# The last cross-attention on explicit keys and values with tiled matmuls, and keys laid out by place modulo 16

## The reference

```
q = xn @ Wq;  k, v = split(ctx @ Wkv)            # 128 -> 1024 = 16 heads x 64
k = concat([nk, k]);  v = concat([nv, v])        # the null key and value
q = l2norm(q) * q_scale;  k = l2norm(k) * k_scale
sim = einsum('bhid,bhjd->bhij', q, k) * 8
out = einsum('bhij,bhjd->bhid', softmax(sim), v)
return layer_norm(out @ Wout, g_out)
```

## Time and profile before

| | |
|---|---|
| median of 3 executions | 1432.56 us (1431.87 to 1434.22) |
| the profiled execution, first to last instruction (span) | 1431.2 us |
| what lies around the span, against the median | 1.4 us |
| PE busy | 1246.7 us, 87% |
| DVE, ACT, POOL busy | 643.0, 439.2, 314.3 us |

### The profile page before, as it was taken

How to read it: one execution, slowest core, us unless ns; L and a number is a source line. 1 busy time by engine, 2 the same in 40 slices (tenths; PEclk the granted TensorE clock), 3 DMA queues, 4 the chain that set the end, 5 groups by cost and what they waited for, 6 DMA issues and landing times.

```text
span 1431.2 us, 12934 instructions
## 1 busy us (share of the span) xinstructions
PE 1246.7 (87%) x4726; PEld 723.7 (51%) x4726; DVE 643.0 (45%) x1098; ACT 439.2 (31%) x550; POOL 314.3 (22%) x94
## 2 busy tenths in 40 slices
PE   7999768896969998777598699999999999999558
PEld 5766423462656664345278444445445444543534
DVE  2167666214447885522342334344444343443334
ACT  2255340431326554033210432222232222223011
POOL 0000000000000000000000046664664566466000
PEclk8799869996689999689689799999999999999569
DMA  8000000002000002001400000000000000000100
GB/s 350 33 1 0 1 0 0 0 1 118 0 1 1 1 1 89 0 0 37 184 1 1 0 8 22 18 15 16 19 20 14 17 21 15 15 19 7 59 7 7
DMA packets 21365, 40.02 MB, mean 28 GB/s; under 512 B 2496, under 2 KB 18880, under 8 KB 19648
## 3 DMA queue, kind: packets, MB, share of 16 engines
q1 hardware_dynamic: 21312, 39.30, 7.4%
HBM read 39.03 MB, written 0.26 MB: 27 GB/s over the span
## 4 chain that ended last, share of the span: by engine, by line
PE 80%; DVE 11%; ACT 5%; issue 2%; POOL 1%; DMA 0%; POOLq 0%; DVEq 0%; ACTq 0%
PE PSUM L1814 15%; PE PSUM L1818 15%; PE PSUM L1389 8%; PE PSUM L1460 4%; PE PSUM L1398 3%; PE PSUM L1421 3%; PE PSUM L1451 2%; PE PSUM L1549 2%; PE PSUM L1560 2%; PE PSUM L1474 2%; PE PSUM L1415 2%; PE PSUM L1849 1%; PE PSUM L1924 1%; DVE ARENA L867 1%; PE PSUM L1843 1%
## 5 line engine op out<-in xcount | busy, mean ns | idle before, releaser
L420 POOL TENSOR_TENSOR ARENA<-ARENA 128x2048 f32<-128x2048 f32 x64 | 288.7, 4510 | 196.5 <-ACT ARENA L654 196.5
L1230 DVE TENSOR_TENSOR ARENA<-PSUM,RK 128x512 f32<-128x512 f32 x256 | 175.5, 690 | 272.5 <-PE PSUM L1814 270.1
L1814 PE MATMUL PSUM<-ARENA,CK 128*128 128x512 f32 x512 | 258.5, 608 | 5.2 <-DVE ARENA L1230 4.2
L1818 PE MATMUL PSUM<-ARENA,CK 128*128 128x512 f32 x512 | 253.8, 598 | 5.8 <-ACT ARENA L676 3.7
L654 ACT ACTIVATE ARENA<-ARENA,CK 128x2048 f32<-128x2048 f32 x64 | 128.1, 2002 | 349.8 <-DVE ARENA L1230 349.8
L1818 PEld LDWEIGHTS PSUM<-ARENA,CK 128*128 128x128 f32 x512 | 97.5, 191 | 131.9 <-issue 113.4
L1814 PEld LDWEIGHTS PSUM<-ARENA,CK 128*128 128x128 f32 x512 | 98.1, 195 | 127.9 <-issue 97.7
L363 POOL TENSOR_TENSOR RSTD<-VE,MHALF 128x4 f32<-128x4 f32 x17 | 17.1, 1009 | 612.3 <-DVE VE L721 612.3
L1389 PE MATMUL PSUM<-WK,CT 128*128 128x512 f32 x256 | 122.4, 600 | 0.0
L450 ACT ACTIVATE SQ<-PSUM 128x512 f32<-128x512 f32 x128 | 76.3, 597 | 83.5 <-PE PSUM L1389 75.7
L743 DVE TENSOR_REDUCE RK<-SQ 128x8 f32<-128x512 f32 x128 | 84.0, 681 | 14.2 <-ACT SQ L450 12.2
(11 more groups left out here) (362 smaller groups left out, 1576.3 us busy)
## 6 DMA issues: line engine op xcount, KB each, us to landing
CT<-in_ctxT SPq DMA_DIRECT2D x4, 1024.0 KB, 10.2
CK<-in_l0f_experts SPq DMA_DIRECT2D x1, 4096.0 KB, 22.8
CK<-in_ctxk SPq DMA_DIRECT2D x1, 4096.0 KB, 12.2
ARENA<-in_l2f_experts SPq DMA_DIRECT2D x2, 2048.0 KB, 8.1
CK<-in_ctxT SPq DMA_DIRECT2D x64, 64.0 KB, 1.7
CK<-in_ctxr SPq DMA_DIRECT2D x64, 64.0 KB, 1.8
ARENA<-in_l2f_experts SPq DMA_DIRECT2D x1, 3072.0 KB, 14.1
WB<-in_wb SPq DMA_DIRECT2D x1, 2738.5 KB, 11.2
```

Source lines behind the costliest of these rows:

```text
L420: nc.gpsimd.tensor_tensor(LS[b % 2], LS[b % 2], PR[:, k % 2, :], ALU.add)\
L1230: ve.tensor_tensor(PR[:, k % 2, c * 512:(c + 1) * 512].rearrange("p (j n) -> p j n", j=4), PSUM[:, c % 2, :].rearrange("p (j n) -> p j n", ...
L1814: mm(bank(c % 2), CTT[:, k, :], qpb[:, b, c * 512:(c + 1) * 512], start=True, stop=True)\
L1818: return mm(bank(4 + c), CKT[:, k, :], PR[:, k % 2, c * 512:(c + 1) * 512], start=first, stop=final, skip_group_check=True)
```

## The change

It does seven things.

1. **Order of the context rows.** Within a batch, row 16m + s now stands at place 128s + m. `CTB` and `KSB` become contiguous: a head's 128 rows are neighbours. The mask is laid out likewise.
2. **No key-norm passes** in the two cores: L1389, L450, L743 go, and the square root and reciprocal of RK with them.
3. **No folded queries** (L1802, L650) and no loads of context tiles in the last block; it reads CT, which no other block overwrites now.
4. **Explicit keys.** For each group of four tiles (512 rows) 8 matmuls of 512 columns (`key_rows`), each copied by ACT into KG and squared by ACT into KSQ. Then 8 matmuls with 32 output rows each (`add_squares`, one per 128 inner features, placed in four column strips of PE) sum the squares, DVE copies them (`key_norms`), four transposes turn them (`turn_norms`), DVE copies 128x64 into RK, and POOL raises 128x64 to -0.5 (`key_scales`).
5. **Explicit values.** Two matmuls of 512 columns for each tile (`value_rows`), copied by DVE.
6. **Tiled matmuls.** Scores of a tile are 16 matmuls of 64 rows, 128 columns, heads 2c and 2c+1 in the upper and the lower 64 rows of PE, into different banks; values are 16 matmuls of 64 output rows, alternately in the two column halves of PE, accumulated in banks 6 and 7, already turned, so `finish_values` and `finish_turn` go. The null key and value are matmuls as well.
7. **The loop** of 64 tiles is written out. Banks 2 to 5 hold scores, 6 and 7 values; all else takes banks 0 and 1 in turn.

The core of the diff:

```diff
+        CTB = CT[:, :].rearrange("p (b s m) -> p b s m", b=B, s=H)
+        KSB = KS.rearrange("p (b s m) -> p b s m", b=B, s=H)
...
+            def key_scales(g):
+                nc.gpsimd.wait_ge(sem("l3x_squares_turned"), PO.due("l3x_squares_turned"))
+                nc.gpsimd.tensor_tensor(RK[:, g % 2, :], RK[:, g % 2, :], MHALF[:, :], ALU.pow)\
+                    .then_inc(sem("l3x_key_scales"), PO.sends("l3x_key_scales"))
+            key_scales(0)
+            for t in range(TILES):
+                b = t // KEY_TILES
+                if t % KEY_TILES == 0:
+                    nc.gpsimd.wait_ge(sem("l3x_l_begun"), PO.due("l3x_l_begun"))
+                nc.gpsimd.wait_ge(sem("l3x_probs"), PO.due("l3x_probs", n=2))
+                nc.gpsimd.tensor_tensor(LS[b % 2], LS[b % 2], PR[:, t % 2, :], ALU.add)\
+                    .then_inc(sem("l3x_summed"), PO.sends("l3x_summed"))
+                nc.gpsimd.wait_ge(sem("l3x_summed"), PO.sent("l3x_summed"))
+                if norm_work(t):
+                    key_scales(t // 4 + 1)
...
+            def probs(t, half):
+                nc.scalar.wait_ge(sem("l3x_scores_taken"), AC.due("l3x_scores_taken", n=2))
+                p = PR[:, t % 2, half * 1024:(half + 1) * 1024]
+                act(p, p, ACT.Exp, bias=SHIFT).then_inc(sem("l3x_probs"), AC.sends("l3x_probs"))
+            probs(0, 0)
+            probs(0, 1)
+            for t in range(TILES):
+                keys = key_work(t)
+                if t and t % KEY_TILES == 0:
+                    nc.scalar.wait_ge(sem("l3x_values"), t)
+                    nc.scalar.wait_ge(sem("l3x_out_kept"), t // KEY_TILES - 1)
+                    act(OT8, PSUM[:, 6:8, :].rearrange("p c n -> p (c n)"), ACT.Copy).then_inc(sem("l3x_o_kept"), AC.sends("l3x_o_kept"))
+                if keys:
+                    key_rows(*keys[0])
+                if t + 1 < TILES:
+                    probs(t + 1, 0)
+                for k in keys[1:]:
+                    key_rows(*k)
+                if keys:
+                    key_squares(*keys[0])
+                if t + 1 < TILES:
+                    probs(t + 1, 1)
+                for k in keys[1:]:
+                    key_squares(*k)
...
+            def key_norms(g):
+                nc.vector.wait_ge(sem("l3x_squares_added"), DV.due("l3x_squares_added"))
+                ve.tensor_scalar(NRM[:, :], bank(work_n[g]), 1e-24, None, ALU.max).then_inc(sem("l3x_squares_kept"), DV.sends("l3x_squares_kept"))
+            def key_norms_turned(g):
+                nc.vector.wait_ge(sem("l3x_norms_turned"), DV.due("l3x_norms_turned"))
+                if g >= 2:
+                    nc.vector.wait_ge(sem("l3x_scores_taken"), 16 * (g - 1))
+                src = PSUM[:, work_t[g], :].rearrange("p (t j r) -> p (t j) r", t=4, j=4)[:, :, 0:4]
+                ve.tensor_copy(RK[:, g % 2, :].rearrange("p (a r) -> p a r", r=4), src)\
+                    .then_inc(sem("l3x_squares_turned"), DV.sends("l3x_squares_turned"))
+            def scale(t, q):
+                k = t % 2
+                if q % 2 == 0:
+                    nc.vector.wait_ge(sem("l3x_scores"), 2 * t + q // 2 + 1)
+                if q == 0:
+                    if t >= 2:
+                        nc.vector.wait_ge(sem("l3x_values"), t - 1)
+                        nc.vector.wait_ge(sem("l3x_summed"), t - 1)
+                    if t % 4 == 0:
+                        nc.vector.wait_ge(sem("l3x_key_scales"), t // 4 + 1)
+                r, i = q // 2, q % 2
+                rk = RK[:, (t // 4) % 2, :].rearrange("p (t j x) -> p t j x", t=4, j=4)[:, t % 4, :, 2 * r + i]
+                ve.tensor_tensor(PR[:, k, q * 512:(q + 1) * 512].rearrange("p (j n) -> p j n", j=4),
+                                 PSUM[:, 2 + q, :].rearrange("p (j n) -> p j n", j=4), each(rk, P), ALU.mult)\
+                    .then_inc(sem("l3x_scores_taken"), DV.sends("l3x_scores_taken"))
+            def value_rows(t, half):
+                nc.vector.wait_ge(sem("l3x_value_rows"), DV.due("l3x_value_rows"))
+                if t >= 2 and half == 0:
+                    nc.vector.wait_ge(sem("l3x_values"), t - 1)
+                ve.tensor_copy(VT[:, t % 2, half * 512:(half + 1) * 512], bank(work_v[2 * t + half]))\
+                    .then_inc(sem("l3x_value_rows_kept"), DV.sends("l3x_value_rows_kept"))
+            def begin_sums(b):
+                if b >= 2:
+                    nc.vector.wait_ge(sem("l3x_l"), b - 1)
+                ve.tensor_scalar(LS[b % 2], PN, w("l3x_first")[:, b:b + 1], None, ALU.mult)\
+                    .then_inc(sem("l3x_l_begun"), DV.sends("l3x_l_begun"))
             def finish_sums(b):
+                nc.vector.wait_ge(sem("l3x_l"), b + 1)
+                ve.reciprocal(L9INV[:, 0:512], bank(0))
+                ve.reciprocal(L9INV[:, 512:1024], bank(1)).then_inc(sem("l3x_l_kept"), DV.sends("l3x_l_kept"))
                 nc.vector.wait_ge(sem("l3x_l_kept"), DV.sent("l3x_l_kept"))
+                nc.vector.wait_ge(sem("l3x_o_kept"), b + 1)
+                ve.tensor_tensor(OT8, OT8, L9INV, ALU.mult).then_inc(sem("l3x_o_ready"), DV.sends("l3x_o_ready"))
             def finish_out(b):
+                nc.vector.wait_ge(sem("l3x_out"), b + 1)
+                ve.tensor_copy(OAT[:, b, :], PSUM[:, work_o[b], 0:P]).then_inc(sem("l3x_out_kept"), DV.sends("l3x_out_kept"))
...
+            for t in range(TILES):
+                more = t + 1 < TILES
+                begins = more and (t + 1) % KEY_TILES == 0
+                ends = t and t % KEY_TILES == 0
+                if more:
+                    scale(t + 1, 0)
+                    scale(t + 1, 1)
+                if t and t % KEY_TILES == 1:
+                    finish_out(t // KEY_TILES - 1) if t > 1 else None
+                for what in norm_work(t):
+                    if what == "added":
+                        key_norms(t // 4 + 1)
+                if more:
+                    value_rows(t + 1, 0)
+                    scale(t + 1, 2)
+                    scale(t + 1, 3)
+                    value_rows(t + 1, 1)
+                if norm_work(t):
+                    key_norms_turned(t // 4 + 1)
+                if begins:
+                    begin_sums((t + 1) // KEY_TILES)
+                if ends:
+                    finish_sums(t // KEY_TILES - 1)
             finish_sums(B - 1)
...
+            def add_squares(g):
+                k = work_n[g]
+                take(k)
+                nc.tensor.wait_ge(sem("l3x_key_squares"), 8 * (g + 1))
+                for c in range(8):
+                    j = c % 4
+                    last = mm(PSUM[32 * j:32 * j + 32, k, :], w("l3x_pick")[:, 32 * (c // 4):32 * (c // 4) + 32], KSQ[c],
+                              start=c < 4, stop=c >= 4, skip_group_check=True)
+                last.then_inc(sem("l3x_squares_added"), PE.sends("l3x_squares_added"))
+                freed[k] = ("l3x_squares_kept", g + 1)
...
+            def scores(t):
+                b, g = t // KEY_TILES, t // 4
+                if t % 4 == 0:
+                    nc.tensor.wait_ge(sem("l3x_key_rows_kept"), 8 * (g + 1))
+                for half in range(2):
+                    if t:
+                        nc.tensor.wait_ge(sem("l3x_scores_taken"), 4 * (t - 1) + 2 * half + 2)
+                    for j in range(4):
+                        c = 4 * half + j
+                        for i in range(2):
+                            last = mm(PSUM[:, 2 + 2 * half + i, j * P:(j + 1) * P],
+                                      KG[DH * i:DH * (i + 1), g % 2, c, (t % 4) * P:(t % 4 + 1) * P],
+                                      QSC[DH * i:DH * (i + 1), c, b * P:(b + 1) * P], start=True, stop=True)
+                    last.then_inc(sem("l3x_scores"), PE.sends("l3x_scores"))
+            def null_values(b):
+                if b:
+                    nc.tensor.wait_ge(sem("l3x_o_kept"), b)
+                for q in range(4):
+                    i = q % 2
+                    mm(PSUM[DH * i:DH * (i + 1), 6 + q // 2, :], w("l3x_nvr")[32 * b:32 * b + 1, :],
+                       PN[32 * b:32 * b + 1, q * 512:(q + 1) * 512], start=True, stop=False, skip_group_check=True)
+            def values(t):
+                nc.tensor.wait_ge(sem("l3x_probs"), 2 * t + 2)
+                nc.tensor.wait_ge(sem("l3x_value_rows_kept"), 2 * t + 2)
+                for c in range(8):
+                    for i in range(2):
+                        at = ((c // 4) * 2 + i) * 512 + (c % 4) * P
+                        last = mm(PSUM[DH * i:DH * (i + 1), 6 + c // 4, (c % 4) * P:(c % 4 + 1) * P],
+                                  VT[:, t % 2, (2 * c + i) * DH:(2 * c + i + 1) * DH], PR[:, t % 2, at:at + P],
+                                  start=False, stop=t % KEY_TILES == KEY_TILES - 1, skip_group_check=True)
+                last.then_inc(sem("l3x_values"), PE.sends("l3x_values"))
...
+            scores(0)
+            for t in range(TILES):
```

(26 more changed lines are left out.)

467 lines of the change are left out of this document (176 added, 291 removed).

## The result

The changed kernel takes 1494.0 us (median of 4 runs, 1490.3 to 1498.6), the kernel before 1432.3 us beside it: a ratio of 1.042, with a 95% interval of 1.041 to 1.044. That is 62 us slower. The forecast had the direction and said 1535, 103 us slower: 41 us too much.

The account below looks back on a forecast made before the run. The prediction took PE, busy for 87% of the span, as the bound. Its terms summed as 1431.2 - 12 - 14 - 5 + 0 + 141 - 7.6 = 1533.6, plus 1.4 outside the span: 1535 us, range 1425 to 1625.

Parts of the forecast that it names:

- Context rows as neighbours: Prologue: value passes over strided context rows get faster once rows are neighbours; saves 12 us, bounds 0 and 18.
- Key norms leave the cores: L0 and L1 cores: groups without key norms run at half clock, 5.6 us each; saves 14 and 5 us.
- the cores keep the full clock: Rival, L0 and L1 cores: clock stays full, 37 + 37 us off, 1461 us; chance 0.15.
- Start of the last block: Before the last block's loop: added and removed work balance; 0 us, bounds -5 and +8.
- Loop: Last block's loop of 64 tiles: 635 us against 494, so +141 us.
- power's stall: Loop: POOL's 10.2 us power delays its add, then DVE and PE; 3.0 us, 14 times, 42 us.
- clock falls: Loop: 8 us in the sum for falls of the clock, as the price of waits at batch ends.
- ends of batches: Three inside the loop: sums, null values, output matmuls and waits for DVE's reciprocals; 11 x 3 = 33 us.
- Column halves pair: Loop values and squares: forecast assumed pairing; the rival that they do not pair said 1670 us, chance 0.10.
- The power isn't short: Loop, POOL: forecast took 10.2 us for the power; the rival of a short power said 1485 us, chance 0.12.
- PE is held by no other engine: Rival, loop: other engines' lateness never reaches PE, under 8.3 us a tile, 1427 us; chance 0.17.
- Tail: After the loop, to the last output: 17.8 us in place of 25.4, so -7.6 us.

Follow-up runs that it names:

- experiment 3: Kernel before with only the change's layout of keys, context and mask (by place modulo 16): 1409.3 us, ratio 0.982.
- experiment 5: Changed kernel with score rows swapped between the cores, 8 of 128 rows in L0 and 128 in place of 8 in L1: 1499.5 us.
- experiment 4: Changed kernel with the keys back in their old order, all else as changed: 1532.0 us.
- experiment 8: Changed kernel with POOL's power in four parts (1416 us), plus each tile's values done lower output half first, then upper, not alternately: 1490.5 us.

## Why the prediction was right, and where its size was off

**Context rows as neighbours:** 16 for 12 us. Three batches gain 3.3 us and the fourth 2.4, at a lower clock, 12 in all; the rest is what the bound of 18 allowed for, a higher clock in the matmuls between (experiment 3).

**Key norms leave the cores: the step that failed, for the L0 core.** The prediction read that "nothing in the new group makes the clock rise" from stretches of other short work (rows 7, 8). For L1 it held: 5.6 us forecast, 5.61 measured, clock 0.50; that the last digit fits is luck, for the scores took 2.0 us for 1.9 and the values 1.8 for 1.9. In L0 the clock was back at 1.00 from 60.5 us and the group took 3.17, nearer to the 3.3 that the text had worked out for the full clock. Its rival "the cores keep the full clock" came true by half, 37 of its 74 us. Two things bear on it, and both stood in the rows. The scores of L0 work over 128 rows and those of L1 over 8 (the shapes in rows 5); swapping only that swapped the clocks (experiment 5; why 8 rows should matter, or whether it is the change of tile shape that comes with them, stays open). And the layout took the stride out of L0's scores, 1.97 to 1.14 us; with the stride left in, the clock changes all through the core (experiment 4). The prediction priced the layout in the prologue and left the strided scores to this step, where the half clock made them worth nothing (16 strided passes 3.80 us at half clock, 16 with neighbours 3.78 here); it is worth 24 us before the change and up to 38 in it.

**Start of the last block:** +2.6 for 0, inside -5 to +8.

**Loop:** 630 for 635 us, but some terms cancel.

| term | forecast | measured |
|---|---|---|
| plain tiles, 64 | 370 | 371 (5.80 each) |
| key rows and bank waits | 103 + 26 | 112 |
| squares and turns, 15 | 48 | 36 |
| power's stall, 14 | 42 | 70 (5.0 each) |
| clock falls | 8 | in the line above |
| ends of batches, 3 | 33 | 27 |
| fill and the rest | 5 | 14 |

The measured column is from the tile distances: a group takes 8.6 + 7.7 + 8.2 + 8.6 = 33.1 us with the power in parts; less 4 x 5.8 and 2.4 that is 7.5 for eight key rows, 0.94 each, 120 of them. The bank waits were about 1 us a group smaller than thought. The power was forecast at 10.2 us from two shapes and took 10.55; the stall on TensorE at 3.0 and took 3.2; what was missing is that each stall pulls the clock down behind it (1.8 us, 14 times: 25). No run shows the 8 us that the loop's sum has for falls of the clock as the price of the waits at the ends of batches. In the kernel before, the clock fell at each of the three ends, but behind 32 passes of one moving column each (L1843), and the only wait of TensorE near them is 1.24 us; in the kernel after it fell behind waits of 3.20 us, once a group. An end: 15.3 + 9.6 - 7.7 - 8.2 = 9.0 us. The rest, 14, is what remains of 630; 7.6 of it are the first group's power (19.2 us for 11.5 in parts). That the loop came out 5 us off is thus partly luck: stalls and clock were 20 us under-sized together, squares and bank waits 29 us over-sized.

**Rivals.** Column halves pair (experiment 8), so 1670 is out. The power isn't short. "PE is held by no other engine" needed under 8.3 us a tile: with the power in parts the loop comes to about 556 us, 8.7 a tile, so even then it would not have held in the loop; that the kernel beats the one before all the same (1416) is due to the 70 us gained ahead of the loop.

**Tail:** -6.1 for -7.6.

The loop still costs more than it did before: 556 us against 494. Whether the old loop with all gains ahead of it would be faster than 1382 us wasn't tried; its key norms need a place, and in the kernel before they are what fills both cores.
